# Linear attention with a routed feed-forward layer: four runs of 64-row matmuls in a step instead of three, and the projections of pk in the middle

## The chip, the cores and the metric

The kernel runs on one core of one Trainium2 chip. The metric is the device time of one execution in microseconds (us); three runs of the kernel before have a median of 726.92 us. The engines are named as the profile names them: PE (TensorE, matmul), PEld (its weight loads), DVE (VectorE), ACT (ScalarE), POOL (GpSimd) and SP (SyncE). Each runs its own list of instructions in order, and they meet only at semaphores.

## The reference, cut to what matters

One transformer layer with adaptive layer norm. The input x is 4 sequences of 1024 tokens of width 128. Its first half is causal linear attention with 16 heads of 64:

```python
phi(x) = exp(x @ omega.T - 0.5 * sum(x * x)) / sqrt(64)      # per head
out = sum over earlier tokens s of (phi_q[t] . phi_k[s]) v[s]
z   = 1 / (sum over s of phi_q[t] . phi_k[s] + 1e-6)
x   = x + ga * ((out * z) @ wo.T + bo)
```

Its second half normalises again, picks two of eight experts for each token by a softmax over `h @ wg`, finds each token's place in its experts, and runs the experts (128 to 512 to 128, with gelu). The change touches the first half and the routing that is woven into it; the experts come after it.

## The kernel before, in words

The 4096 tokens are 32 chunks (NCH) of 128, eight (CPB) to a sequence. The attention is a loop of steps, written out, one for each chunk c (with two short ones behind it); j is the chunk's number in its sequence. In a step the engines work on several chunks: the projections (q, k, v, pq, pk; line 263) are of chunk c+1, the attention of chunk c, the last half of the heads, their transposes and the output projection (`add_heads`, line 521) of chunk c-1, and the routing of chunk c-2. The projections' weights pq and pk are wq and wk already multiplied with omega.

Within a chunk the causal sum is made of two halves of 64 tokens. Four functions make it, each twice in a step, for the heads' pairs 0 to 3 (g = 0) and 4 to 7 (g = 1). Each call issues 16 matmuls of 64 rows and 64 columns, which use a quarter of the array each; an fp32 matmul shows as two weight loads and two matmul records, so a call is 32 of each (half as many at the ends of a sequence, in two of the functions):

- `score(g)`, line 299: keys against queries. When the call for g = 1 is through, both banks are ready (`a0_in`, `a1_in`), and DVE multiplies them with the mask (`mask`, line 857).
- `attend_state(g)`, line 318: queries against the running state. Its last matmul counts up `o_begun`.
- `attend(g)`, line 337: masked scores against values, added onto the same sums. It waits until `o_begun` tells that its own `attend_state(g)` is through (line 343).
- `state_gain(g)`, line 354: what the chunk adds to the state. DVE adds it in `state_add(g)` (line 882) with two instructions, first `mid`, then `state` (one instruction when j is 7), and then counts up `gain{g}_out`.

All other matmuls use the whole array. In the order of the step of PE (lines 553 to 610) the 64-row matmuls stand in three runs: run A is `attend_state(1)` and `attend(1)` of chunk c-1 with `state_gain(0)` of chunk c between them (96 weight loads), run B is `score(0)` and `score(1)` (64), run C is `attend_state(0)`, `state_gain(1)`, `attend(0)` (96). Behind run C stand the two small matmuls of `routing_rank`, the projections of pk, and `add_heads`. `add_heads` waits for the copies of the transposed heads (`attT0_out`, `attT1_out`) and, since its bank is also that of `state_gain(1)`, for `gain1_out` of the same chunk (lines 522 to 525):

```python
pe.wait_ge(sem("attT0_out"), c)
pe.wait_ge(sem("attT1_out"), c)
if c < NCH:
    pe.wait_ge(sem("gain1_out"), c + 1)
```

The orders of ACT (line 698) and DVE (line 852) are written out by hand as well. DVE adds the state, divides the heads by their sums (`normalise`, line 864), masks the scores, forms the exponents of phi (`exponent`, line 763), makes the first layer norm (`first_norm`, line 143) and picks the experts (`choose`, line 901). ACT squares, copies out of PSUM, takes the exponentials (`exps`, line 624) and copies the transposed heads (line 738). POOL forms the second layer norm and, once a step, sends the chunk's rows to their places with two indirect DMAs (`scatter`, line 1103, issued on line 1108). SP issues nothing in the steps that the change touches.

Of the kernel before, what the change touches and what calls it, by code (L numbers as in the profile page):

```python
# [33 lines left out]
def build(nc, x, omega, wq, wk, wv, wo, bo, wg, w1, b1, w2, b2, cond, wmod, out):  # L34
# [26 lines left out]
    with ExitStack() as ctx:  # L61
# [92 lines left out]
        def attention():  # L154
            with ExitStack() as tmp:
# [104 lines left out]
                with nc.Block(no_gpsimd_drain=True) as block:  # L260
                    @block.tensor
                    def _(pe):
# [55 lines left out]
                        def attend_state(g, c, par, j):  # L318


                            if g == 0:
                                if c >= 2:
                                    pe.wait_ge(sem("lg_out"), c - 1)
                            else:
                                for z in range(2):
                                    pe.wait_ge(sem(f"o{z}_out"), c + 1)
                            pe.wait_ge(sem(f"gain{g}_out"), c + 1)
                            for i in range(4):
                                for side in range(1 if j == 0 else 0, 2):
                                    for z in range(2):  # L330
                                        r = half_rows(z)
                                        mm = pe.matmul(out(i, z, side), phiT["q"][par][r, 4 * g + i, half_rows(side)],  # L332
                                                       (mid if side else state[par])[r, 4 * g + i, :],
                                                       start=(i == 0), stop=False, skip_group_check=True)
                            mm.then_inc(sem("o_begun"), 1)
# [217 lines left out]
                        def step(c, b, j):  # L553
# [22 lines left out]
                            state_gain(0, c, par, j)  # L576
                            if tail:
                                attend(1, c - 1, nxt, (j - 1) % CPB)
                            if front:
                                project("v0", c, nxt)  # L580
                                project("v1", c, nxt)
                            score(0, c, par)
                            score(1, c, par)
                            if last:
                                routing_T(c, par)
                            if live(c, 2):
                                pe.wait_ge(sem("gain0_out"), c + 1)
                                pe.wait_ge(sem("xn_ready"), c + 3)
                                pe.transpose(psum[BANK["hT"]][:, 0:P], xn[par][:], ident[:]).then_inc(sem("hT_in"), 1)
# [3 lines left out]
                            if last:  # L593
                                routing_logits(c)
                            if tail:
# [4 lines left out]

                            attend_state(0, c, par, j)
# [4 lines left out]
                            if front:  # L606
                                project("pk0", c, nxt)
                                project("pk1", c, nxt)
# [6 lines left out]
                    def _(act):  # L615
# [82 lines left out]
                        def step(c, b, j):  # L698
# [30 lines left out]
                            if last and c != NCH:  # L729
                                rows_out()  # L730
                            if live(c, 2):
                                shift_scale(c, b, j, par)
                            if last and c != NCH:
                                logits_out()
# [8 lines left out]
                            if front:  # L743
                                exps("q", c, nxt)
# [12 lines left out]
                    def _(dve):  # L757
# [94 lines left out]
                        def step(c, b, j):  # L852
# [135 lines left out]
                            if back:  # L988
                                state_add(0)
                            if tail:  # L990
                                normalise(1, c - 1)
                            if back:
                                mask(0)
                                mask(1)
                            if front:
                                exponent("q", 0, c)
                                exponent("q", 1, c)
                            if live(c, 3):
                                first_norm(dve, c + 3, nxt)
                            if last and c != NCH:  # L1000
                                choose()
# [6 lines left out]
                            if front:  # L1008
                                exponent("k", 0, c)
                                exponent("k", 1, c)  # L1010
# [503 lines left out]
```

## Time and profile before

| | us |
|---|---|
| median of three runs | 726.92 |
| the profiled execution | 727.18 |
| its span, first to last instruction | 725.1 |
| PE busy | 697.4 |
| DVE busy | 536.0 |
| ACT busy | 387.6 |
| POOL busy | 335.6 |

The profile lists each engine's instructions with start and duration. Durations of matmuls are modelled, and those of neighbours overlap; for PE the distance from one start to the next is what counts. The loop of steps fills the span from about 30 to 570 us; the experts fill the rest.

### The profile page before, as it was taken

How to read it: one execution, taken by the hardware profiler on the slowest of the kernel's cores; microseconds unless marked ns; L12 is line 12 of the kernel's file. 1: busy time of each engine (PE TensorE's matmuls, PEld its weight loads, DVE VectorE, ACT ScalarE, POOL GpSimd, SP SyncE). 2: the span in 40 equal slices, each digit the busy share in tenths (PEclk: the TensorE clock that was granted, in tenths of full speed). 3: DMA queues.
4: the chain of work that ended last, by engine and by line, in shares of the span. 5: the costliest groups of instructions: out<-in, count | busy, mean ns of one | idle time of the engine just before them, and what ended most of it. 6: DMA issues, size and time to landing. Idle time of an engine off the chain costs nothing. (4 is left out here: it accounts for less than half of the span.)

```text
span 725.1 us, 27349 instructions
## 1 busy us (share of the span) xinstructions
PE 697.4 (96%) x11452; PEld 604.1 (83%) x11452; DVE 536.0 (74%) x1685; ACT 387.6 (53%) x740; POOL 335.6 (46%) x625
## 2 busy tenths in 40 slices
PE   8999999999999999999999999999999789999956
PEld 8788888888888888888888888888887779999942
DVE  6687888878878887888878878888775456565416
ACT  5755566665656665666656566665552144544310
POOL 3002545555544445454545554545447306556550
PEclk9999999999999999999999999999999999999989
DMA  9974000000000000000000000000000154553128
GB/s 252 362 268 178 11 9 11 10 9 11 14 15 10 11 10 11 10 10 11 9 11 11 14 14 9 11 11 11 10 11 14 49 177 130 168 173 113 51 82 304
DMA packets 32705, 47.25 MB, mean 65 GB/s; under 512 B 4132, under 2 KB 20168, under 8 KB 32584
## 3 DMA queue, kind: packets, MB, share of 16 engines
q1 hardware_dynamic: 23296, 32.62, 13.4%
q0 software_dynamic: 4096, 8.42, 3.6%
q10 hardware_dynamic: 5192, 4.47, 1.9%
q8 instruction: 91, 1.49, 0.9%
q14 instruction: 30, 0.25, 0.1%
HBM read 22.21 MB, written 23.36 MB: 63 GB/s over the span
## 5 line engine op out<-in xcount | busy, mean ns | idle before, releaser
L1297 POOL DMA_INDIRECT y_rows<-y_sb,row_id x64 | 62.8, 982 | 66.0 <-DVE y_sb L1442 49.9
L1108 POOL DMA_INDIRECT dispatched<-h_cur,slot x64 | 67.3, 1051 | 17.8 <-issue 16.1
L1376 ACT ACTIVATE hidden<-bank,b_col 128x512 f32<-128x512 f32 x64 | 43.3, 689 | 58.2 <-PE bank L1348 57.8
L632 ACT ACTIVATE phi_k<-expo_k 128x1024 f32<-128x1024 f32 x32 | 33.9, 1058 | 74.5 <-DVE expo_k L768 70.7
L648 ACT COPY v_sb<-bank 128x512 f32<-128x512 f32 x64 | 37.6, 587 | 62.1 <-PE bank L279 58.7
L527 PEld LDWEIGHTS bank<-woT,attT 128*128 128x128 f32 x512 | 61.9, 192 | 3.2 <-ACT attT L738 0.6
L859 DVE TENSOR_TENSOR scores<-bank,within 128x512 f32<-128x512 f32 x64 | 41.2, 686 | 31.2 <-PE bank L310 31.2
L527 PE MATMUL bank<-woT,attT 128*128 128x128 f32 x512 | 62.4, 275 | 0.4 <-ACT attT L738 0.4
L1317 PE MATMUL bank<-w_sb,hidden 128*128 128x128 f32 x512 | 59.7, 275 | 0.8 <-issue 0.8
L137 POOL TENSOR_TENSOR rs<-var,power 128x1 f32<-128x1 f32 x64 | 37.1, 579 | 49.8 <-DVE var L132 49.5
L1317 PEld LDWEIGHTS bank<-w_sb,hidden 128*128 128x128 f32 x512 | 58.3, 192 | 1.2 <-issue 1.2
L768 DVE SCALAR_TENSOR_TENSOR expo_k<-norm_k,bank 128x512 f32<-128x512 f32 x64 | 43.9, 687 | 16.5 <-PE bank L279 16.0
L1038 POOL TENSOR_TENSOR h_lo<-h_full,h_hi 128x192 fp32r<-128x192 f32 x32 | 19.0, 594 | 79.2 <-ACT h_hi L641 79.2
L878 DVE TENSOR_TENSOR att<-bank,rden 128x256 f32<-128x256 f32 x128 | 48.3, 419 | 2.2
L348 PE MATMUL bank<-v_sb,scores 64*64 64x65 f32 x2048 | 48.4, 220 | 0.8 <-issue 0.8
L621 ACT ACTIVATE square_q<-bank 128x512 f32<-128x512 f32 x64 | 38.1, 600 | 17.9 <-PE bank L279 17.1
L760 DVE TENSOR_REDUCE norm_k<-square_k 128x16 f32<-128x1024 f32 x32 | 39.0, 1219 | 10.2 <-ACT square_k L621 10.1
L332 PE MATMUL bank<-mid,phiT_q 64*64 64x65 f32 x1024 | 43.7, 224 | 0.0
L738 ACT COPY attT<-bank 128x512 f32<-128x512 f32 x64 | 34.4, 589 | 17.4 <-PE bank L388 17.4
L375 PE MATMUL bank<-v_sb,phi_k 64*64 64x65 f32 x1920 | 43.1, 218 | 0.0
L348 PEld LDWEIGHTS bank<-v_sb,scores 64*64 64x64 f32 x2048 | 41.3, 134 | 2.0 <-issue 1.1
L768 DVE SCALAR_TENSOR_TENSOR expo_q<-norm_q,bank 128x512 f32<-128x512 f32 x64 | 42.2, 682 | 0.3 <-issue 0.3
(243 smaller groups left out, 2037.9 us busy)
## 6 DMA issues: line engine op xcount, KB each, us to landing
dispatched<-blank SPq DMA_DIRECT2D x16, 524.0 KB, 3.1
region<-dispatched SPq DMA_DIRECT2D x30, 262.0 KB, 2.9
y_rows<-blank SPq DMA_DIRECT2D x8, 512.0 KB, 3.9
w_nat<-in_L_ffn_w_dram SPq DMA_DIRECT2D x8, 256.0 KB, 3.7
y_got<-y_rows SPq DMA_DIRECT2D x8, 256.0 KB, 6.8
y_got<-y_rows ACTq DMA_DIRECT2D x8, 256.0 KB, 7.4
out_dram<-x_sb SPq DMA_DIRECT2D x8, 256.0 KB, 3.7
w_sb<-in_L_ffn_w_dram ACTq DMA_DIRECT2D x6, 256.0 KB, 2.8
```

Of the source, the lines that this page charges most:

```text
L332: mm = pe.matmul(out(i, z, side), phiT["q"][par][r, 4 * g + i, half_rows(side)], (mid if side else state[par])[r, 4 * g + i, :], start=(i ...
L348: mm = pe.matmul(out(i, z, side), scores[keys, (2 * g + z) * 4 + i, :], v_sb[par][keys, 8 * z + 4 * g + i, :], start=(j == 0 and side == 0 ...
L375: mm = pe.matmul(psum[bank][half_rows(z), i * VW:(i + 1) * VW], phi["k"][par][toks, h * M:(h + 1) * M], v_sb[par][toks, 8 * z + 4 * g + i, :],
L527: mm = pe.matmul(psum[BANK["wo"]][:, 0:D], attT[:, t, :], woT[:, t, :], start=(t == 0), stop=(t == NP - 1))
L760: dve.tensor_reduce(norm[k][:], square[k][:].rearrange("p (h d) -> p h d", d=DH), AX, ALU.add).then_inc(sem(f"norm_{k}_ready"), 1)
L768: dve.scalar_tensor_tensor(out=expo[k][:].rearrange("p (t z m) -> p z t m", z=2, m=M)[:, half], in0=norm[k][:, half * 8:half * 8 + 8].unsq ...
L859: dve.tensor_tensor(scores[:].rearrange("p (g y i) t -> p y g (i t)", g=2, y=2)[:, z], psum[BANK[f"a{z}"]][:].rearrange("p (g x) -> p g x" ...
L878: dve.tensor_tensor(heads[:, z], o[:, :, 0:DH], rden[g][:, z, :].unsqueeze(2).to_broadcast([P, 4, DH]), ALU.mult)\
L1108: pool.indirect_dma_start(out=dispatched[:, :], in_=h2_cur[par][:], in_offset=None, out_offset=bass.IndirectOffsetOnAxis(ap=slot[par][:, k ...
L1297: pool.indirect_dma_start(out=y_rows[:, :], out_offset=bass.IndirectOffsetOnAxis(ap=row_id[par][:, t:t + 1].bitcast(U32), axis=0), in_=y_s ...
L1317: mm = pe.matmul(psum[bank][:, t * D:(t + 1) * D], hidden[par][:, k, t * P:(t + 1) * P], w2_sb[w][:, k, :], start=(k == 0), stop=(k == KH ...
L1376: act.activation(hidden[par][:, k, :], psum[2 + k][:], ACT.Gelu, bias=b1_col[:, bass.ds(e * KH + k, 1)]).then_inc(sem(f"hid{k}_out"), 1)
```

## The change

In PE's order, `attend(1)` follows `attend_state(1)` directly, `state_gain(0)` goes behind the projections of v and ahead of `score(0)`, `score(1)` goes behind the routing's logits and ahead of `attend_state(0)`, the transpose hT, then pk's projections, then the transposes of the heads follow, and `state_gain(1)` and `attend(0)` come last but for the rank and `add_heads`. The four runs are so: `attend_state(1)`, `attend(1)`; `state_gain(0)`, `score(0)`; `score(1)`, `attend_state(0)`; `state_gain(1)`, `attend(0)`. `attend_state(0)` gets two more waits, for `o2_out` and `o3_out`; hT loses its wait for `gain0_out`. ACT copies the logits ahead of scaling the rows, and takes the exponentials of q ahead of the copies of the transposed heads. DVE gets an order to match: the exponents of q ahead of the masks, those of k ahead of `state_add(1)`.

```diff
@@ attend_state, g == 0
                                 if c >= 2:
                                     pe.wait_ge(sem("lg_out"), c - 1)
+                                if c >= 1:
+                                    for z in range(2):
+                                        pe.wait_ge(sem(f"o{2 + z}_out"), c)
@@ PE, step
                             if tail:
                                 attend_state(1, c - 1, nxt, (j - 1) % CPB)
-                            state_gain(0, c, par, j)
-                            if tail:
                                 attend(1, c - 1, nxt, (j - 1) % CPB)
                             if front:
                                 project("v0", c, nxt)
                                 project("v1", c, nxt)
+                            state_gain(0, c, par, j)
                             score(0, c, par)
-                            score(1, c, par)
                             if last:
                                 routing_T(c, par)
-                            if live(c, 2):
-                                pe.wait_ge(sem("gain0_out"), c + 1)
-                                pe.wait_ge(sem("xn_ready"), c + 3)
-                                pe.transpose(psum[BANK["hT"]][:, 0:P], xn[par][:], ident[:]).then_inc(sem("hT_in"), 1)
                             if front:
                                 project("pq0", c, nxt)
                                 project("pq1", c, nxt)
                             if last:
                                 routing_logits(c)
+                            score(1, c, par)
+                            attend_state(0, c, par, j)
+                            if live(c, 2):
+                                pe.wait_ge(sem("xn_ready"), c + 3)
+                                pe.transpose(psum[BANK["hT"]][:, 0:P], xn[par][:], ident[:]).then_inc(sem("hT_in"), 1)
+                            if front:
+                                project("pk0", c, nxt)
+                                project("pk1", c, nxt)
                             if tail:
                                 attended_T(0, c)
                                 attended_T(1, c)
                             if c == 0:
                                 pe.wait_ge(sem("woT_ready"), 2)
-
-                            attend_state(0, c, par, j)
                             state_gain(1, c, par, j)
                             attend(0, c, par, j)
                             if last:
                                 routing_rank(c)
-                            if front:
-                                project("pk0", c, nxt)
-                                project("pk1", c, nxt)
                             if tail:
                                 add_heads(c)
@@ ACT, step
                             if last and c != NCH:
                                 rows_out()
+                            if last and c != NCH:
+                                logits_out()
                             if live(c, 2):
                                 shift_scale(c, b, j, par)
-                            if last and c != NCH:
-                                logits_out()
+                            if front:
+                                exps("q", c, nxt)
                             if tail:
                                 for half in range(2):
                                     act.wait_ge(sem(f"attT{half}_in"), c)
...
-                            if front:
-                                exps("q", c, nxt)
@@ DVE, step
                             if front:
                                 sum_squares("k", c)
-                            if back:
-                                state_add(0)
                             if tail:
                                 normalise(1, c - 1)
                             if back:
-                                mask(0)
-                                mask(1)
+                                state_add(0)
                             if front:
                                 exponent("q", 0, c)
                                 exponent("q", 1, c)
+                            if back:
+                                mask(0)
+                                mask(1)
+                            if last and c != NCH:
+                                choose()
                             if live(c, 3):
                                 first_norm(dve, c + 3, nxt)
-                            if last and c != NCH:
-                                choose()
+                            if front:
+                                exponent("k", 0, c)
+                                exponent("k", 1, c)
                             if back:
                                 state_add(1)
                             if c == NCH + 1:
                                 last_weights()
                             if last and c != NCH:
                                 find_places()
-                            if front:
-                                exponent("k", 0, c)
-                                exponent("k", 1, c)
                             if back:
                                 normalise(0, c)
```

## Rows read from the trace of the kernel before

**Rows 1.** The page, part 1: busy time of each engine.
```profile
PE 697.4 (96%) x11452; PEld 604.1 (83%) x11452; DVE 536.0 (74%) x1685; ACT 387.6 (53%) x740; POOL 335.6 (46%) x625
```

**Rows 2.** Waits of PE, longest within the steps: engine, line, waited for: total, times, longest.
```profile
PE bank L518 <- DVE hot L914: 2.0, 1, 2.0
```

**Rows 3.** Timeline of PE in one step: start us, us, engine, line, what, count.
```profile
328.47 0.60 PE L296 MATMUL bank<-ident,phi_q 128*128 128x128 f32 x4
328.91 0.60 PE L296 MATMUL bank<-ident,phi_k 128*128 128x128 f32 x4
329.44 0.27 PE L332 MATMUL bank<-state,phiT_q 64*64 64x65 f32 x2
...
329.91 0.22 PE L332 MATMUL bank<-mid,phiT_q 64*64 64x65 f32 x2
329.95 0.65 PE L375 MATMUL bank<-v_sb,phi_k 64*64 64x65 f32 x32
330.42 0.88 PE L348 MATMUL bank<-v_sb,scores 64*64 64x65 f32 x32
331.23 0.50 PE L277 MATMUL bank<-wv_hi,h_hi 128*128 128x512 f32 x1
...
332.82 1.16 PE L310 MATMUL bank<-phiT_q,phiT_k 64*64 64x64 f32 x64
333.91 0.33 PE L507 MATMUL bank<-ident,h_cur 128*128 128x128 f32 x1
...
334.10 0.48 PE L277 MATMUL bank<-wpq_hi,h_hi 128*128 128x512 f32 x1
...
335.57 0.28 PE L511 MATMUL bank<-wg_sb,h2T 128*128 128x8 f32 x2
335.71 1.07 PE L388 MATMUL bank<-ident,att 128*128 128x128 f32 x8
336.71 0.28 PE L332 MATMUL bank<-state,phiT_q 64*64 64x65 f32 x2
...
338.28 0.18 PE L518 MATMUL bank<-hot,tri 128*128 128x16 bf16 x1
```

**Rows 4.** Timeline of PE, attend(1) at the end of run A in three other steps.
```profile
96.64 0.89 PE L348 MATMUL bank<-v_sb,scores 64*64 64x65 f32 x32
...
381.89 0.65 PE L348 MATMUL bank<-v_sb,scores 64*64 64x65 f32 x32
...
531.99 0.88 PE L348 MATMUL bank<-v_sb,scores 64*64 64x65 f32 x32
```

**Rows 5.** Timeline of POOL, the first scatter beside run A, in two steps.
```profile
330.32 1.12 POOL L1108 DMA_INDIRECT dispatched<-h_cur,slot  x1 [0.20 <-issue]
...
382.47 1.13 POOL L1108 DMA_INDIRECT dispatched<-h_cur,slot  x1 [0.49 <-issue]
```

**Rows 6.** Timeline of DVE, same step as rows 3; in brackets its idle time before.
```profile
334.03 1.29 DVE L859 TENSOR_TENSOR scores<-bank,within 128x512 f32<-128x512 f32 x2 [0.98 <-PE bank L310]
335.24 1.32 DVE L768 SCALAR_TENSOR_TENSOR expo_q<-norm_q,bank 128x512 f32<-128x512 f32 x2
...
337.95 0.43 DVE L893 SCALAR_TENSOR_TENSOR mid<-bank,state 128x260 f32<-128x260 f32 x1 [0.18 <-PE bank L375]
338.41 0.43 DVE L897 SCALAR_TENSOR_TENSOR state<-bank,mid 128x260 f32<-128x260 f32 x1
...
339.41 1.38 DVE L768 SCALAR_TENSOR_TENSOR expo_k<-norm_k,bank 128x512 f32<-128x512 f32 x2 [0.40 <-PE bank L279]
```

**Rows 7.** Timeline of ACT, same step.
```profile
336.38 1.07 ACT L738 COPY attT<-bank 128x512 f32<-128x512 f32 x2 [0.32 <-PE bank L388]
337.35 1.07 ACT L632 ACTIVATE phi_q<-expo_q 128x1024 f32<-128x1024 f32 x1
```

**Rows 8.** Timeline of all engines in the closing steps, where PE waits for ACT.
```profile
561.57 0.27 ACT L710 COPY h2T<-bank 128x128 f32<-128x128 f32 x1 [2.31 <-PE bank L507]
...
561.89 0.30 PEld L511 LDWEIGHTS bank<-wg_sb,h2T 128*128 128x128 f32 x2 [0.59 <-ACT h2T L710]
```

## The prediction

> **What bounds the kernel now.** First the busy times: PE works 96% of the span, no other engine more than 74% [rows 1]. A busy PE need not be a PE at its limit, so next PE's waits: inside the steps the longest is one single wait of 2.0 us [rows 2]; nothing recurs from step to step. So every step is PE's own list of instructions, and the same spot of two steps 26 apart, 96.64 and 531.99, gives 16.74 us a step [rows 4]. Whatever makes that list longer, or makes PE wait, goes into the time in full, once for each of some 30 steps. DVE and ACT matter only where PE comes to wait for them.
>
> Third, PE's timeline of one step, read from start to start [rows 3]. Run A goes from 329.44 to 331.23, 1.79 us; run B (64 loads) from 332.82 to 333.91, 1.09; run C, 96 loads like A, from 336.71 to 338.28, 1.57. So A takes 0.22 more than C for as many loads. Where it loses this: its `attend(1)` shows 0.88 and 0.89 us, but 0.65 in the step at 381.89 [rows 3, 4]. Of the 27 full steps from c = 4 to 30, 20 look like the first, seven like the other. Beside the long one a scatter of POOL begins at 330.32, just ahead of `attend(1)`; in the step with the short one it begins at 382.47, when `attend(1)` has been issued [rows 3 to 5]. I read the loss as one of PE's supply of instructions while POOL sends, not of the run's length.
>
> **The change, part by part.** The matmuls, and the DMAs, are the same in number; order and waits differ.
>
> *One run more.* Each run begins and ends with something that a run of 128-row matmuls doesn't have. Ahead of run A four transposes take 0.53 (328.91 to 329.44) instead of 0.44 (328.47 to 328.91): 0.09 to go in [rows 3]. Inside, 32 loads take 0.47 (329.95 to 330.42), 64 would take 0.94, and run B takes 1.09: 0.15 to get out. Four runs like B are 4 x 1.09 = 4.36; A without its loss, B and C are 1.57 + 1.09 + 1.57 = 4.23. So +0.13 inside the runs, +0.09 for the entry. The two transposes behind run B cost 0.19 together (333.91 to 334.10); now each stands behind a run of its own, and one alone costs between 0.11 (a transpose's pitch, 0.44 / 4) and the 0.19 of both, so +0.03 to +0.19. I take +0.08, nearer the low end, since the time to get out of a run is already in the 0.15. Together +0.30 a step, 30 steps: **+9.0 us**. Nothing hides it, as PE is the bound.
>
> *attend(1) right behind attend_state(1).* Until now `state_gain(0)` stood between, so that the wait for `o_begun` was over when its turn came. Now `attend(1)` is due 0.51 us after the run's start (329.95 - 329.44), but `attend_state(1)` issues its last matmul at 329.91 and is through at 330.13 [rows 3]. From a release to PE's next load I take 0.05: ACT ends at 561.57 + 0.27 = 561.84, PE loads at 561.89 [rows 8]. So `attend(1)` starts at 330.19 - 329.95 = 0.24 late, with the projections of v and all that follow queued behind it. 31 steps: **+7.4 us**. Ends: 0, if the last matmul reports at its start, and 0.5 a step, if the instructions behind the wait come as slowly as in the long `attend(1)`.
>
> *The loss beside the scatter* stays, I think: relative to the step POOL's chain is unchanged, and `attend(1)` is still being issued when the scatter begins 0.88 us after the run's start (330.32 - 329.44). I count no change; the ends are 20 x 0.23 = 4.6 us less, if it goes, and 3 more, if it comes in every step.
>
> *add_heads waits for gain1_out.* This is the largest term. `state_gain(1)` now opens the last run, and behind it come only `attend(0)` and the rank's two small matmuls. In run C `state_gain(1)` begins 0.51 behind the run's start, at 337.22; DVE starts `mid` at 337.95, 0.73 later, and ends `state` at 338.41 + 0.43 = 338.84, 1.62 us after the first matmul of `state_gain(1)` [rows 3, 6]. Counted from the start of the new last run, `gain1_out` comes at 1.62 and PE goes on at 1.67; PE would be ready at 1.09 and a little. That is 0.55 of idle PE at best, as DVE can't be earlier than its input. Is DVE free then? Its list now has masks, `choose`, `first_norm` and both exponents of k ahead of `state_add(1)`. Before, masks, exponents of q, `first_norm`, `choose` took from 334.03 to 337.95, of which 0.18 idle: 3.74; the exponents of k (1.38) take the place of those of q (1.32), so 3.80 [rows 6]. The masks start when `score(1)` is through: 334.03 - 332.82 = 1.21 behind run B's start, and 0.47 less where `score(1)` opens the run, so 0.74 into the third run. DVE is free 0.74 + 3.80 = 4.54 after the third run's start. PE begins the last run after 1.09 (run) + 0.15 (hT) + 1.47 (pk, by pq's 334.10 to 335.57) + 1.00 (attT, 335.71 to 336.71) = 3.71, and DVE's input is there 0.73 later, at 4.44 [rows 3]. A near tie; DVE is 0.1 late. So the stall is between 0.55 and 0.65; I take 0.6. In 27 of the steps: 16.2; in the three with j = 7 one DVE instruction (0.46) is absent and 0.14 is left: 0.4. **+16.6 us.** What queues behind: `add_heads` and with it the next step's start.
>
> *Moved with one answer: no cost.* pk's projections want pq's banks free: the exponents of q follow pq at once and end about 0.6 before pk's turn, behind the third run (1.09) and hT. ACT now takes the exponential of q (1.07) ahead of the copies of the heads (1.07) [rows 7]; the copies then end some 0.3 before the rank asks for them, the thinnest cover of all; if it is gone, the loss falls into the same idle time before `add_heads` and costs nothing until it exceeds 0.6. The two new waits of `attend_state(0)` are for divisions that end about 3 us earlier. POOL's list is unmoved, and no queue of DMAs is touched.
>
> Sum: 9.0 + 7.4 + 16.6 = 33.0. The profiled execution (727.18) lies 0.26 above the median of 726.92; from the median, **760 us**.
>
> **The rivals.**
>
> *Only the extra run counts* (7%). If `o_begun` comes early and `gain1_out` is hidden too, 726.9 + 9.0 = 736, or 731 with the scatter's loss gone. Against it: the 0.73 and two times 0.43 stand in the trace of today.
>
> *gain1_out is hidden, the other two are not* (10%): 726.9 + 16.4 = 743. It needs `add_heads` to start while the state is being added, and its own wait speaks against it.
>
> *Faster* (5%). A run loses time by its length: when more than 64 loads stand in a row, PE's supply of instructions runs out, as at the end of run A; runs of 64 end before that. If run C lost as much as A, splitting both would save 2 x 0.23 x 30 = 13.8, and with both waits hidden the time is 726.9 + 9.0 - 13.8 = 722. It decides if the waits cost under 0.16 a step together. Against it: run C with its 96 loads shows no such loss, nor does A in the seven steps. The Trainium skill (TensorE: Matmul & The Clock Gate, the table at its head) gives the engine a queue of 64 with a partial reorder window, which would make 64 the length that counts; the trace disagrees so far, since run C keeps the pitch of B to its end at 1.57 us.
>
> *DVE becomes late by another 0.5* (8%), because an instruction among masks, `choose` and `first_norm` waits for something that the trace doesn't show: + 0.5 x 27 = 13.5, so 774.
>
> *The prices cancel* (3%): the scatter's loss goes (-4.6), entries overlap, waits are hidden; 727. That the change doesn't do what it says can be left out: the order of the calls gives four runs of two calls each, 64 loads.
>
> **How the numbers follow.** The forecast with all three terms has 67%, and its own range from the terms' ends is 752 to 770. The range over the cases, 741 to 774, takes in the second and most of the fourth rival, and leaves out the first, the third and the fifth, 15%, and some tails. About 0.2% (1.5 us) is what a measurement of this kernel can tell from no change: faster 5%, same 3%, slower 92%.
>
> **What would show it.** Right: PE's waits get a line of `add_heads` (L527) on DVE's state, about 0.5 us at a time and some 14 to 17 in total; `attend(1)` starts about 0.75 after its run's start; four runs of about 1.1 (the first longer) in a step of some 17.9; PE's share falls to about 92%. DVE and ACT keep their busy times. Wrong: no idle PE ahead of `add_heads`, or steps of 17.2 or less; above all, runs of 64 loads that take under 1.0 us.

## The result, and the profile after

| | us, median | lowest to highest | runs |
|---|---|---|---|
| before | 727.02 | 726.3 to 727.3 | 4 |
| changed | 766.50 | 765.25 to 769.88 | 4 |

The ratio is 1.0552, with a 95% interval of 1.0516 to 1.0587: 39.5 us slower. The rows below come from the run of 769.88 (span 767.9, granted clock 0.986, the other three 0.992 or 0.993); all differences of times are taken between medians.

The page of the changed kernel, part 1 and one group of part 5 (busy us, mean ns of one, then the idle time before it with its releaser):

```profile
PE 715.7 (93%) x11452; PEld 611.7 (80%) x11452; DVE 544.6 (71%) x1685; ACT 386.5 (50%) x740; POOL 335.0 (44%) x625
...
L530 PE MATMUL bank<-woT,attT 128*128 128x128 f32 x512 | 64.7, 280 | 22.3 <-DVE state L897 20.9
```

PE did as many instructions as before [rows 1], and its share fell from 96% to 93%. ACT and POOL kept their busy times; DVE took 8.6 us more for as many instructions, a hint that e9 comes back to. So PE has begun to wait, and the page names the place: `add_heads`, now on line 530. The waits of PE have the same line on top, and it was absent before [rows 2] (total us, times, longest):

```profile
PE bank L530 <- DVE state L897: 20.9, 27, 1.1
...
PE bank L530 <- DVE mid L893: 1.0, 3, 0.3
```

27 are the steps with two instructions in `state_add(1)`, and the 3 are steps with one (j is 7). Next, one whole step by the view of windows (window, its length, busy us of PE, PEld, DVE, ACT and POOL, clock, DMA share, GB/s):

```profile
340.39:358.44 18.05, 17.18 (x334) 14.61 (x333) 14.17 (x46) 10.14 (x20) 8.48 (x17) 1.00 0.03 10
```

A step takes 18.05 us instead of 16.74 [rows 4], at the full granted clock; over the same 26 steps the mean is 17.98 (101.71 to 569.24). The timeline of PE says where; first the second half of that step (start, us; the last row is cut off by the end of the window, the call has 16 matmuls):

```profile
340.39 0.28 PE L514 MATMUL bank<-wg_sb,h2T 128*128 128x8 f32 x2
340.61 0.69 PE L310 MATMUL bank<-phiT_q,phiT_k 64*64 64x64 f32 x32
...
341.70 0.33 PE L596 MATMUL bank<-ident,xn 128*128 128x128 f32 x1
341.78 0.47 PE L277 MATMUL bank<-wpk_hi,h_hi 128*128 128x512 f32 x1
...
343.26 1.03 PE L391 MATMUL bank<-ident,att 128*128 128x128 f32 x8
344.22 0.70 PE L378 MATMUL bank<-v_sb,phi_k 64*64 64x65 f32 x32
...
345.32 0.18 PE L521 MATMUL bank<-hot,tri 128*128 128x16 bf16 x1
345.36 0.17 PE L522 MATMUL bank<-hot,ones 128*128 128x16 bf16 x1
346.31 0.91 PE L530 MATMUL bank<-woT,attT 128*128 128x128 f32 x6 [0.79 <-DVE state L897]
```

The third run (`score(1)`, `attend_state(0)`) goes from 340.61 to 341.70, 1.09; the last (`state_gain(1)`, `attend(0)`) from 344.22 to 345.32, 1.10. Behind the rank's two matmuls stands a hole of 0.79. Then the first two runs, the spot that answers to run A [rows 3]:

```profile
352.79 0.28 PE L335 MATMUL bank<-state,phiT_q 64*64 64x65 f32 x2
...
353.26 0.22 PE L335 MATMUL bank<-mid,phiT_q 64*64 64x65 f32 x2
353.57 0.70 PE L351 MATMUL bank<-v_sb,scores 64*64 64x65 f32 x32
354.20 0.50 PE L277 MATMUL bank<-wv_hi,h_hi 128*128 128x512 f32 x1
...
355.79 0.70 PE L378 MATMUL bank<-v_sb,phi_k 64*64 64x65 f32 x32
356.31 0.64 PE L310 MATMUL bank<-phiT_q,phiT_k 64*64 64x64 f32 x32
356.88 0.33 PE L510 MATMUL bank<-ident,h_cur 128*128 128x128 f32 x1
356.97 0.48 PE L277 MATMUL bank<-wpq_hi,h_hi 128*128 128x512 f32 x1
```

The first run takes 354.20 - 352.79 = 1.41, the second 1.09. In the first, `attend(1)` starts 0.31 after the last matmul of `attend_state(1)` has started, where the next call inside a run otherwise starts after 0.04 (329.91 to 329.95 in [rows 3]). Once begun, `attend(1)` keeps its pace: it is 0.63 to the projections of v, where run A took 0.81 (330.42 to 331.23 in [rows 3]). The scatter is still beside it, 353.66 - 352.79 = 0.87 after the run's start; it was 0.88 before [rows 3, 5]:

```profile
353.66 1.12 POOL L1108 DMA_INDIRECT dispatched<-h_cur,slot  x1 [0.20 <-issue]
```

### The profile page after: what moved, and what is told of

It is laid out like the page before. It is cut to its first block and busy times, and to the rows that moved or that the text cites. A ratio compares the mean times of both kernels' runs of the same rounds, so it can differ in the third digit from the quotient of the medians.

```text
span 767.9 us, 27349 instructions
## 1 busy us (share of the span) xinstructions
PE 715.7 (93%) x11452; PEld 611.7 (80%) x11452; DVE 544.6 (71%) x1685; ACT 386.5 (50%) x740; POOL 335.0 (44%) x625
## 5 line engine op out<-in xcount | busy, mean ns | idle before, releaser
L530 PE MATMUL bank<-woT,attT 128*128 128x128 f32 x512 | 64.7, 280 | 22.3 <-DVE state L897 20.9
L530 PEld LDWEIGHTS bank<-woT,attT 128*128 128x128 f32 x512 | 59.6, 191 | 24.6 <-issue 24.0
L768 DVE SCALAR_TENSOR_TENSOR expo_q<-norm_q,bank 128x512 f32<-128x512 f32 x64 | 43.8, 687 | 20.4 <-PE bank L279 20.3
L378 PEld LDWEIGHTS bank<-v_sb,phi_k 64*64 64x64 f32 x1920 | 36.0, 134 | 17.0 <-ACT v_sb L648 10.9
L351 PE MATMUL bank<-v_sb,scores 64*64 64x65 f32 x2048 | 43.9, 222 | 2.7
L378 PE MATMUL bank<-v_sb,phi_k 64*64 64x65 f32 x1920 | 44.9, 224 | 0.0
L310 PE MATMUL bank<-phiT_q,phiT_k 64*64 64x64 f32 x2048 | 43.2, 221 | 0.0
L768 DVE SCALAR_TENSOR_TENSOR expo_k<-norm_k,bank 128x512 f32<-128x512 f32 x64 | 41.0, 675 | 3.0 <-PE bank L279 3.0
L893 DVE SCALAR_TENSOR_TENSOR mid<-bank,state 128x260 f32<-128x260 f32 x56 | 23.6, 421 | 26.8 <-PE bank L378 26.7
```

The source lines that it names most:

```text
L310: mm = pe.matmul(psum[BANK[f"a{z}"]][keys, col:col + HALF], phiT["k"][0][r, 4 * g + i, keys], phiT["q"][par][r, 4 * g + i, half_rows(side) ...
L351: mm = pe.matmul(out(i, z, side), scores[keys, (2 * g + z) * 4 + i, :], v_sb[par][keys, 8 * z + 4 * g + i, :], start=(j == 0 and side == 0 ...
L378: mm = pe.matmul(psum[bank][half_rows(z), i * VW:(i + 1) * VW], phi["k"][par][toks, h * M:(h + 1) * M], v_sb[par][toks, 8 * z + 4 * g + i, :],
L530: mm = pe.matmul(psum[BANK["wo"]][:, 0:D], attT[:, t, :], woT[:, t, :], start=(t == 0), stop=(t == NP - 1))
L768: dve.scalar_tensor_tensor(out=expo[k][:].rearrange("p (t z m) -> p z t m", z=2, m=M)[:, half], in0=norm[k][:, half * 8:half * 8 + 8].unsq ...
```

## The experiments

All nine were timed beside the kernel before on the same chip, and a difference below is to that. Line numbers shift a little between kernels; the names stay.

| experiment | starts from | us, median | before | ratio, 95% interval |
|---|---|---|---|---|
| e1 | changed | 740.48 | 727.73 | 1.0176, 1.0155 to 1.0196 |
| e2 | changed | 762.22 | 727.73 | 1.0480, 1.0455 to 1.0504 |
| e3 | before | 727.43 | 727.73 | 0.9996, 0.9983 to 1.0009 |
| e4 | before | 739.15 | 727.73 | 1.0157, 1.0130 to 1.0184 |
| e5 | before | 723.37 | 726.86 | 0.9954, 0.9941 to 0.9968 |
| e6 | changed | 760.14 | 726.86 | 1.0456, 1.0436 to 1.0476 |
| e7 | before | 734.50 | 726.86 | 1.0114, 1.0096 to 1.0132 |
| e8 | before | 732.92 | 726.86 | 1.0083, 1.0066 to 1.0099 |
| e9 | changed | 758.45 | 727.29 | 1.0425, 1.0388 to 1.0463 |

**e1: the changed kernel, without what makes add_heads wait.** Its sums go to another bank, that of the heads' transposes, whose last reader is done by then; the waits of the banks' other users follow.

```diff
-                         2: ["tk0", "tk1", "a0", "attT0"], 3: [...],
+                         2: ["tk0", "tk1", "a0", "attT0", "wo"], 3: [...],
...
-                         6: ["late0", "hT", "late1"], 7: ["early0", "early1", "wo"]}
+                         6: ["late0", "hT", "late1"], 7: ["early0", "early1"]}
@@ add_heads
                             pe.wait_ge(sem("attT1_out"), c)
-                            if c < NCH:
-                                pe.wait_ge(sem("gain1_out"), c + 1)
```

> The changed kernel, with the output projection's sums in the bank of attT0 instead of that of early1, so that add_heads no longer waits for gain1_out (tk0 of the next step waits for wo_out in its place, state_gain(0) for gain1_out of the chunk before). Theory: the wait is the largest term, 0.95 us idle and 0.08 of slower first matmuls in 27 steps and about half in three, 28 us; nothing else is late behind it, as the copies of the heads end 0.3 us before the rank: 766 - 28 = 738 us, with PE's idle time ahead of add_heads gone. Rival (DVE is the real bound, its list is only shifted by the wait): another wait on DVE takes its place, at tk0 or in the next step's attend_state, and the time stays above 750.

Measured: 740.48, 12.75 above before, where the changed kernel is 39.5 above. So this wait alone is 26.7 us, two thirds of the loss. PE's timeline at the same spot of a step:

```profile
331.38 0.17 PE L522 MATMUL bank<-hot,ones 128*128 128x16 bf16 x1
331.40 2.03 PE L528 MATMUL bank<-woT,attT 128*128 128x128 f32 x16
```

`add_heads` starts 0.02 after the rank's second matmul; in the changed kernel it is 346.31 - 345.36 = 0.95. The 0.93 between them, in 27 steps, is 25.1, and the three short waits come on top.

**e2: the changed kernel, with state_gain(0) back in front of attend(1).** The first run is run A again, and `score(0)` stands alone.

```diff
                                 attend_state(1, c - 1, nxt, (j - 1) % CPB)
+                            state_gain(0, c, par, j)
+                            if tail:
                                 attend(1, c - 1, nxt, (j - 1) % CPB)
...
-                            state_gain(0, c, par, j)
                             score(0, c, par)
```

> The changed kernel, with state_gain(0) back between attend_state(1) and attend(1): a first run of 96 loads, and score(0) alone behind the projections of v. Theory: the wait for o_begun costs 0.32 a step (first run 1.41 instead of 1.09), so the two runs take 1.56 + 0.63 = 2.19 instead of 2.50, 9.6 us less in 31 steps, if the loss at the end of the run stays away: 757. If the loss comes back with the order (0.23 in 20 steps), 761. Rival (the length of a run costs, not the wait): the first run takes 1.8 in every step, and the time stays at 764 or above.

Measured: 762.22, 34.5 above before, so 5.0 less than the changed kernel. The run and the scatter beside it, first PE, then POOL:

```profile
348.80 0.27 PE L335 MATMUL bank<-state,phiT_q 64*64 64x65 f32 x2
...
349.32 0.65 PE L378 MATMUL bank<-v_sb,phi_k 64*64 64x65 f32 x32
349.79 0.87 PE L351 MATMUL bank<-v_sb,scores 64*64 64x65 f32 x32
350.59 0.50 PE L277 MATMUL bank<-wv_hi,h_hi 128*128 128x512 f32 x1
```

```profile
349.67 1.13 POOL L1109 DMA_INDIRECT dispatched<-h_cur,slot  x1 [0.20 <-issue]
```

The wait is gone (`attend(1)` follows at the usual pitch, 0.47 after `state_gain(0)`), and the loss is back: 0.87, and a run of 1.79 as in [rows 3]. 0.32 won in 31 steps is 9.9, 0.23 lost in 20 is 4.6: this exchange should give 5.3, and 5.0 came (either ratio is known to some 2 us, so the times agree with the two terms, but it is the rows that show them).

**e3: the kernel before, with the scatter meant to come behind run A.**

```diff
                                 pool.wait_ge(sem("slot_ready"), c - 1)
+                                if live(c, 1):
+                                    pool.wait_ge(sem("v0_in"), c + 2)
```

> The kernel before, with POOL's scatter held until the projection of v0 has been issued, which is behind run A. Theory (the loss at the end of run A comes from the scatter that begins beside it): run A takes 1.56 in all steps, 20 x 0.23 = 4.7 us less, 722.4. Rival (the length of the run, or its place in the step): run A stays at 1.79 and the time at 727.

Measured: 727.43 to 727.73, the same. The experiment is void, since the count chosen was that of a v long projected: the scatter still began 0.91 after the run's start (330.57, the run at 329.66), and the run still took its 1.8. It says nothing for or against either theory.

**e4: the kernel before, with one run more and nothing else.** The transpose h2T (`routing_T`) goes between `score(0)` and `score(1)`.

```diff
                             score(0, c, par)
-                            score(1, c, par)
                             if last:
                                 routing_T(c, par)
+                            score(1, c, par)
```

> The kernel before, with the transpose of the routing between score(0) and score(1): four runs, without any new wait. Theory: one run more costs 0.15 inside the runs and 0.07 to enter it, 0.2 a step in 30 steps: 727 + 6 = 733. Rival (a run of at most 64 loads is no worse than a longer one, and the price of a run is only its matmuls): 727 to 728.

Measured: +11.4 us, more than expected. PE's timeline:

```profile
321.27 0.69 PE L310 MATMUL bank<-phiT_q,phiT_k 64*64 64x64 f32 x32
321.89 0.33 PE L507 MATMUL bank<-ident,h_cur 128*128 128x128 f32 x1
322.15 0.69 PE L310 MATMUL bank<-phiT_q,phiT_k 64*64 64x64 f32 x32
322.78 0.33 PE L589 MATMUL bank<-ident,xn 128*128 128x128 f32 x1
322.86 0.48 PE L277 MATMUL bank<-wpq_hi,h_hi 128*128 128x512 f32 x1
```

Two runs of 32 loads take 0.62 + 0.63 = 1.25 instead of 1.09, and the transpose between them takes 0.26, where both together took 0.19 [rows 3]. From the start of `score(0)` to pq it is 1.59 instead of 1.28: 0.31 a step, 9.3 us in 30 steps. In the trace the kernel is 9.6 behind when the experts begin (593.32 against 583.73), and the other 2 come behind them, where PE's granted clock is 0.58 and 0.73 from 707 to 727, against 0.66 and 1.00 in the two stretches that answer before (697.4 to 717.4). So a single small instruction between two runs costs more than its own time; I read this as paying for the way out and the way in at once.

**e5: the scatter behind run A, this time in fact.** One count later than in e3.

```diff
                                 pool.wait_ge(sem("slot_ready"), c - 1)
+                                if live(c, 2):
+                                    pool.wait_ge(sem("v0_in"), c + 3)
```

> The kernel before, with POOL's scatter held until the next step's projection of v0 has been issued (the experiment before it asked for the v0 of the step before, which is long done when the scatter's turn comes, so that nothing moved). The scatter should begin some 2.7 us behind the start of run A instead of 0.89. Theory (the loss at the end of run A needs the scatter's beginning beside it): run A takes 1.56 in all steps, 4.7 us less, 722.5. Rival (the loss belongs to a run of more than 64 loads at this place): run A stays at 1.79 in most steps, 727.

Measured: 723.37, ratio 0.9954 (0.9941 to 0.9968). This is faster than both kernels. PE, then POOL:

```profile
331.38 0.27 PE L332 MATMUL bank<-state,phiT_q 64*64 64x65 f32 x2
...
332.94 0.50 PE L277 MATMUL bank<-wv_hi,h_hi 128*128 128x512 f32 x1
```

```profile
334.78 1.12 POOL L1110 DMA_INDIRECT dispatched<-h_cur,slot  x1 [2.72 <-PE bank L279]
```

The scatter begins 3.40 after the run's start, and run A takes 1.56, as run C does; so it does in every step. The loss at the end of run A needs the scatter beside it. But the scatter beside it is not enough. Of the seven steps of the kernel before in which run A is short, only three have a late scatter (1.17 to 1.56 after the run's start). In three, those with j = 7, `state_gain(0)` has half its matmuls, and nothing is lost with the scatter at its usual place, as here in the kernel before, where it comes 0.89 into a run of 1.56 (PE, PE, POOL):

```profile
279.47 0.27 PE L332 MATMUL bank<-state,phiT_q 64*64 64x65 f32 x2
...
281.03 0.50 PE L277 MATMUL bank<-wv_hi,h_hi 128*128 128x512 f32 x1
...
280.36 1.13 POOL L1108 DMA_INDIRECT dispatched<-h_cur,slot  x1 [0.20 <-issue]
```

The seventh, with j = 1, has half of `attend_state(1)` and the scatter at 0.91; the two other steps of its kind take 1.71 and 1.73. Of 20 x 0.23 = 4.6 us, 3.5 arrive; run B, beside which the scatter now lies, is part of the rest, with 1.13 (334.53 to 335.66) instead of 1.09:

```profile
334.53 1.20 PE L310 MATMUL bank<-phiT_q,phiT_k 64*64 64x64 f32 x64
335.66 0.33 PE L507 MATMUL bank<-ident,h_cur 128*128 128x128 f32 x1
```

**e6: the changed kernel, with the state added ahead of the exponents of k.**

```diff
                                 first_norm(dve, c + 3, nxt)
+                            if back:
+                                state_add(1)
                             if front:
                                 exponent("k", 0, c)
                                 exponent("k", 1, c)
-                            if back:
-                                state_add(1)
```

> The changed kernel, with state_add(1) ahead of the exponents of k in DVE's list. Theory: the wait for gain1_out is 0.95 us because DVE comes 0.34 late to state_add(1) behind masks, choice and exponents; ahead of them it begins when its input is there, and 27 x 0.34 = 9 us go: 757.5, with 0.6 us of idle PE left ahead of add_heads. Rival (the exponents of k, now later, make the next step's tk0 wait): no gain, 766.

Measured: 33.3 above before instead of 39.5, so 6.2 less. The wait that is left:

```profile
PE bank L530 <- DVE state L897: 13.6, 27, 0.6
```

13.6 / 27 = 0.50 a step, with `state_add(1)` as early as its input allows. DVE now stands idle for 0.81 before `mid` (341.77), which starts 0.76 after the last run's start instead of 1.07. So a better order on DVE takes off 0.27 a step, but most of the wait is the two DVE instructions themselves, between the last run and `add_heads`.

**e7: the kernel before, with two runs instead of three.** Run B is joined to A: 160 loads in a row.

```diff
                             state_gain(0, c, par, j)
+                            score(0, c, par)
+                            score(1, c, par)
                             if tail:
                                 attend(1, c - 1, nxt, (j - 1) % CPB)
                             if front:
                                 project("v0", c, nxt)
                                 project("v1", c, nxt)
-                            score(0, c, par)
-                            score(1, c, par)
```

> The kernel before, the other way round: run B joined to run A (attend_state(1), state_gain(0), score(0), score(1), attend(1): 160 loads), so two runs a step. Theory (each run costs 0.25 to 0.31 to enter and to leave, its length nothing): 30 x 0.25 to 0.31 = 7.5 to 9.3 less, 718 to 720, if attend(1) keeps its loss beside the scatter, down to 715 if not. Rival (a run of more than 64 loads loses by its length): the long run loses more than 0.25, and the time is 727 or above.

Measured: 734.50, 7.6 slower; I had expected the other sign, and the rival's time was the right one. Most steps are 0.25 shorter, as one run less should make them. But PE's waits, and one step's timeline, show holes, such as this one inside a long run:

```profile
PE bank L348 <- issue: 6.2, 7, 1.3
```

```profile
369.94 0.55 PE L348 MATMUL bank<-v_sb,scores 64*64 64x65 f32 x21
371.61 0.44 PE L348 MATMUL bank<-v_sb,scores 64*64 64x65 f32 x10 [1.12 <-issue]
```

The hole falls between two matmuls of one call, where nothing is waited for, and the trace puts it down to issue. The kernel before has one such hole within its steps (0.84, in a run C), e5 has three of about 0.5; in the steps of the changed kernel there is one, in the second (1.0). So this order, with its run of 160, does bring holes. With three on lines 277 and 278 there are ten in the steps. But only six of them lie in a long run or right behind it; the other four lie in a run C or right behind it, and that has its 96 loads as before. That the supply of instructions is the cause, and that the holes come when PE's next instructions are being fetched, is only argued: each began 1.2 to 2.1 us after a packet of the instruction queue had started. Nor is the whole loss made of them: 2.2 us of it come between the rank of the last full step and the next (4.3 us behind the kernel before, then 6.6), where PE also waits 1.0 for DVE's `att`.

**e8: the kernel before, with the wait for o_begun put into run A and its length kept.**

```diff
                                 attend_state(1, c - 1, nxt, (j - 1) % CPB)
-                            state_gain(0, c, par, j)
-                            if tail:
                                 attend(1, c - 1, nxt, (j - 1) % CPB)
+                            state_gain(0, c, par, j)
```

> The kernel before, with attend(1) directly behind attend_state(1) and state_gain(0) behind it: run A keeps its 96 loads. Theory: the wait for o_begun costs 0.32 in each of 31 steps; the loss beside the scatter may go, as it did in the changed kernel: run A takes 1.56 + 0.32 = 1.88, 727 + 31 x 0.32 - 4.7 = 732, or 737 with the loss kept. Rival (the wait is hidden and the first run of the changed kernel is long for another reason): 727 or less.

Measured: 732.92, +6.1. PE, then POOL:

```profile
333.56 0.28 PE L332 MATMUL bank<-state,phiT_q 64*64 64x65 f32 x2
...
334.04 0.22 PE L332 MATMUL bank<-mid,phiT_q 64*64 64x65 f32 x2
334.35 0.70 PE L348 MATMUL bank<-v_sb,scores 64*64 64x65 f32 x32
...
335.46 0.50 PE L277 MATMUL bank<-wv_hi,h_hi 128*128 128x512 f32 x1
```

```profile
334.45 1.13 POOL L1107 DMA_INDIRECT dispatched<-h_cur,slot  x1 [0.20 <-issue]
```

The wait costs 0.31 here too (334.04 to 334.35), and the loss is gone, although the run has its 96 loads and the scatter begins 0.89 after its start. The run takes 1.90 instead of 1.57 without the loss; 31 x 0.33 - 4.6 = 5.6 is near the 6.1. So the loss vanishes in this order, with all 96 loads in the run. But the order moves the wait for `o_begun` and `state_gain(0)` at once, and behind the wait only 64 loads follow, so that e8 doesn't tell the wait itself from a shorter stretch without one, or from the place of `attend(1)`. That the scatter now begins just after `attend(1)` has started (334.45 and 334.35), where it began just before (330.32 and 330.42), is no sufficient reason: in the three steps of e2 with j = 1 it also begins 0.05 to 0.07 after, and the run takes 1.71 to 1.77, where without a scatter beside it (46.23) it takes 1.55.

**e9: the changed kernel, with POOL's h_lo kept off DVE's choice of experts.** In the step shown above, `hot` on line 913 took 0.56 beside POOL's `h_lo`. DVE, then POOL, in the changed kernel:

```profile
343.23 0.56 DVE L913 TENSOR_SCALAR hot<-iota_e,best_f 128x8 bf16<-128x8 f32 x1
...
344.09 1.27 DVE L768 SCALAR_TENSOR_TENSOR expo_k<-norm_k,bank 128x512 f32<-128x512 f32 x2
345.29 0.41 DVE L893 SCALAR_TENSOR_TENSOR mid<-bank,state 128x260 f32<-128x260 f32 x1
345.73 0.43 DVE L897 SCALAR_TENSOR_TENSOR state<-bank,mid 128x260 f32<-128x260 f32 x1
```

```profile
343.16 0.60 POOL L1038 TENSOR_TENSOR h_lo<-h_full,h_hi 128x192 fp32r<-128x192 f32 x1 [4.51 <-ACT h_hi L641]
```

`hot` starts at 343.23, 0.07 after `h_lo`, and ends at 343.79, when `h_lo` ends at 343.76. The edit lets `h_lo` begin when `hot` is done:

```diff
                             if live(c, 2):
+                                if last:
+                                    pool.wait_ge(sem("hot_ready"), c - 1)
                                 low(c + 2)
```

> The changed kernel, with POOL's h_lo (L1038) held until DVE has written hot. In the changed kernel DVE's L913 takes 0.56 instead of 0.23 us and ends when POOL's h_lo beside it ends. Theory: that is one part of what the forecast of the wait was short by; without the overlap L913 takes 0.23 again, state_add(1) begins 0.33 earlier and add_heads with it: 27 x 0.33 = 8.9 less, 757.5, the wait on DVE's state from 20.9 to 12 us in all. Rival (L913 is long by itself in the new order, or the time is lost again further down DVE's list): 766.

Measured: 31.2 above before instead of 39.5, 8.3 less. All 32 of these instructions, in the changed kernel and then in e9 (ns, least / median / most):

```profile
L913 DVE TENSOR_SCALAR hot<-iota_e,best_f x32: 230/559/566, 73.3 to 608.5; 128x8 bf16<-128x8 f32 x32
```

```profile
L913 DVE TENSOR_SCALAR hot<-iota_e,best_f x32: 229/231/243, 72.4 to 599.3; 128x8 bf16<-128x8 f32 x32
...
PE bank L530 <- DVE state L897: 13.7, 27, 0.7
```

The median falls from 559 to 231 ns, its value in the kernel before as well, and PE's wait falls from 20.9 to 13.7. In the changed kernel 27 of the 32 are long; 27 x 0.33 is 8.9, and DVE's busy time is 8.6 above before; in e9 it is 536.6, 0.6 above. `mid` starts 0.76 after the last run's start (339.35 - 338.59), as early as in e6, where the same wait is left with `hot` still at 0.56. So this meeting is all of DVE's lateness. In e1, too, 27 of the 32 are long, and there PE has no wait for `state` at all. The Trainium skill (SBUF — State Buffer, Who interferes with whom) says that DVE and GpSimd share one pair of ports, that a tensor_scalar can be among the forms that take it, and that the later one is blocked for the whole of the earlier one's instruction. The two ends at 343.76 and 343.79 agree.

## Why the prediction was right, and by which steps

The sign, the largest term and its mechanism came out; the predicted 760 is 6.5 short, inside the range. The order of the two other costs did not: 9.0 was forecast for the run more and 7.4 for `attend(1)`, and about 5 and 9.9 were measured. Three of the four steps were off in size, and one, the loss beside the scatter, in kind. That 760 is so near is partly luck: two terms were forecast 12.6 too low together and two 8.6 too high, 21 us of error in all.

| step | predicted us | measured us | by |
|---|---|---|---|
| add_heads waits for gain1_out | +16.6 | +26.7 | e1 |
| attend(1) right behind attend_state(1) | +7.4 | +9.9 | timeline, e2, e8 |
| one run more | +9.0 | about +5 | timeline |
| the loss beside the scatter | 0 | -4.6 | timeline, e5, e8 |
| sum | +33.0 | +37.0 of 39.5 | |

The last 2.5 us I have not traced. The changed kernel has a hole of 1.2 in its second step, with issue as releaser; the trace of before has one of 1.2 as well (370.27 to 372.99, a run C of 2.72), so that they about cancel. The sum is of medians, and the traced run isn't one: it is 42.7 above the traced one before. In its closing steps PE's granted clock is 0.58 on average from 589 to 593 and 0.69 from 606 to 617, partly at the lower of its two levels (1.2 GHz); ahead of the first fall PE had stood idle three times, for 0.65, 0.35 and 0.46. Before, the two stretches that answer have 1.00 (548.5 to 552.5) and 0.84 (564.5 to 575). By these averages the lower clock costs this run an estimated 3.4 us more, and the steps with which the table is made lie ahead of it.

*add_heads waits for gain1_out.* This is the term that was missed by most, 26.7 for 16.6. The mechanism was as said: the input `mid` wants, a busy DVE, two instructions, then PE. Masks start 0.74 into the third run (341.35 - 340.61), to the hundredth as predicted. The step that failed is "A near tie; DVE is 0.1 late": `mid` starts 345.29 - 344.22 = 1.07 after the last run's start, where 0.73 was the earliest and 0.83 predicted. Of that 0.24, 0.10 is PE, which reached its last run after 3.61 us instead of 3.71, and 0.14 is DVE, whose list from the masks to `mid` took 3.94 instead of 3.80. The 3.80 had every duration from the step of before, where `h_lo` ran at 335.54, before `choose` was due; in the new order `h_lo` meets `hot`, which adds 0.33, while the exponents of k took 0.18 less than booked. That DVE and ACT keep their busy times, which the prediction gives as a sign of being right, therefore failed for DVE. So the prediction's fourth rival, a late DVE, happened in part, and the cause that it named, "something that the trace doesn't show", was a meeting of two engines that could be worked out: `h_lo` follows hT, and hT now stands behind the third run. Then PE goes on 0.15 after `state` ends (346.16 to 346.31), where the price from [rows 8] was 0.05. What was taken as the cost of a wake-up was that of one place. With `mid` on time and this 0.15, e9 has 0.67 from the rank's second matmul to `add_heads` (339.72 to 340.39): nearly the 0.6 that was forecast, and 0.28 less than the 0.95 of the changed kernel.

*attend(1).* Predicted to start 0.75 after its run's start, it starts 0.78 after (353.57 - 352.79), and the run takes 1.41 instead of 1.09, 0.32 a step for 0.24 (the sum has a slip of 0.01: 330.13 + 0.05 is 330.18). The wait is on work that PE itself has just issued, and it shows in no line of the waits, since the matmuls under way last until 353.26 + 0.22 = 353.48, nearly until `attend(1)` starts; only the starts tell.

*One run more.* Inside the runs +0.15 (four of 1.09 or 1.10, the wait taken out, against 1.56 + 1.09 + 1.57 = 4.22), the entry of the third run +0.08 (340.39 to 340.61 is 0.22, against 0.14 in [rows 3]). Against that, h2T and hT, each behind a run of its own, cost 0.09 + 0.08 where together they cost 0.19, and the transposes of the heads 0.96 instead of 1.00. That is +0.17 a step for the +0.30 of the prediction. The term that was wrong is the +0.08 for the transposes. e4 shows that a price of 0.31 does exist, where one small instruction stands alone between two runs; the change hasn't any such place.

*The loss beside the scatter.* "Stays, I think" was wrong, and so is half of its reason. It isn't the number of loads in the run alone: e8 keeps 96 and loses it. Nor is the scatter enough: e8 and the changed kernel have it 0.87 to 0.89 into the run and lose nothing, and neither do the three steps with j = 7, where the prediction's reading, a scatter that comes late, explains only three of its seven short runs. In the full steps it takes both the scatter's beginning (e5) and an `attend(1)` that is issued without a wait behind 64 other loads (e2 has the loss again). What it is that POOL's sending holds up, and whether the wait itself takes the loss away, stays open; no run here looked at that.

*The faster rival* had its sign wrong for this kernel, but not all of its mechanism. The runs of 64 loads took 1.09 as before, so nothing was won inside a run. Long runs do suffer from time to time: in e7, at 160 loads, several times, at 96 once in a while. The Trainium skill (TensorE: Matmul & The Clock Gate, the table at its head) gives the engine a queue of 64; that a run has trouble just above 64 isn't what run C in [rows 3] and run A in e5 show, each with 96 loads at 1.56 or 1.57.

## What to carry to other kernels

Before a block is moved, ask what it covered: here `state_gain(0)` hid a wait of PE on its own matmuls (0.32 us), and pk's projections hid two DVE instructions behind a shared bank (0.95 us), and each wait was in the code, though in no trace, before the move. When one engine's order is changed, lay the lists of the engines beside it over the new order: a price read from the old trace holds only while the same neighbours run at the same time. In a kernel bound by PE, also look at what other engines begin beside its densest stretch: moving POOL's scatter by 2.5 us was the one edit here that beat the kernel before (e5, 0.46% faster).

## What the runs showed of the hardware that was not expected

- A DVE instruction of 0.23 us takes 0.56 beside a POOL instruction. Where PE waits for nothing behind it, no wait shows for it (e1); here it cost 8.3 us (e9).
- PE's start behind a release by DVE took 0.15 us, against 0.05 behind ACT in [rows 8].
- A transpose alone between two runs of 64-row matmuls takes 0.26 us, but 0.08 or 0.09 between such a run and 128-row work (e4, the changed kernel).
- A scatter that begins beside the last of three full 64-row calls takes 0.23 us from it, and nothing where PE has waited just before (e2, e5, e8) or where the call ahead has half its matmuls (the steps with j = 7).
- With a run of 160 loads in the step, PE stands idle for 0.4 to 1.3 us ten times, in the long runs and in others, with issue as the only releaser that the trace names (e7).
